# Moving the softplus remainder and the delta transposes, and plain DMAs for the mixtures' zero rows

## The reference, cut to what matters

```python
x = x + _L0_ffn_ref(_layernorm(x), ...)        # mixture: 8 experts, 2 for each token
x = x + _L1_attn_ref(_layernorm(x), ...)       # delta rule, 16 heads of 128
x = x + _L1_ffn_ref(_layernorm(x), ...)        # mixture: 8 experts, 2 for each token
# in the delta rule, for each head:
q, k, v = silu(short_conv(x @ W.T))            # three products, 4 taps
e = k @ Wsv.T - v                              # "guess errors"; their norms feed a small MLP
beta, amp = mlp_b(stats), mlp_a(stats)
g = -exp(A_log) * softplus(k / |k| * amp + dt_bias)
# recurrence over the tokens: S = S*exp(g); delta = (v - k.S)*beta; S += k x delta; o = q.S
```

## Time and profile before

| what | value |
|---|---|
| median of the runs | 7040.8 us (7029.47 to 7044.65, 3 runs) |
| profiled execution: its own time, its span | 7044.94 us, 7044.5 us |
| busy share of the span, PE / DVE / ACT / POOL | 81% / 74% / 54% / 40% |
| m0 from its first instruction to its end | 1334.5 to 1885.6 us |
| delta layer's preparation, up to the first projection | 1885.6 to 1995.1 us |
| delta loop, first to last decay | 2043 to 6043 us |
| m1 to the end | 6490.1 to 7044.5 us |

### The profile page before, as it was taken

One profiled execution on the slowest core, in us unless ns is written; L12 is line 12 of the kernel. 1 busy time (PEld: TensorE's weight loads), 2 busy tenths in 40 slices (PEclk: granted clock), 3 DMA queues, 4 the chain that ended last, 5 costly groups with the idle time before them and its releaser, 6 DMA issues. The chain is left out here.

```text
span 7044.5 us, 200500 instructions
## 1 busy us (share of the span) xinstructions
PE 5709.3 (81%) x69344; PEld 4012.6 (57%) x69345; DVE 5182.1 (74%) x11270; ACT 3800.4 (54%) x7867; POOL 2816.5 (40%) x4799
## 2 busy tenths in 40 slices
PE   6878999879167888888888888888888888688483
PEld 4767888645135555555555555555555555577342
DVE  6967777652347888888888888888888888555564
ACT  2324444212045676676676776766766767367121
POOL 2320000130325555555655555565556555200403
PEclk9979999889679999999999999999999999789697
DMA  1000000112300000000000000000000000001213
GB/s 34 0 17 7 4 5 5 44 47 86 84 10 15 16 13 16 16 16 13 13 16 16 16 13 16 13 16 16 16 13 13 16 16 11 11 12 58 75 63 100
DMA packets 136087, 172.77 MB, mean 25 GB/s; under 512 B 29104, under 2 KB 110096, under 8 KB 135184
## 3 DMA queue, kind: packets, MB, share of 16 engines
q1 hardware_dynamic: 122896, 135.34, 6.3%
q0 software_dynamic: 13056, 35.67, 1.6%
HBM read 128.74 MB, written 42.21 MB: 24 GB/s over the span
## 5 line engine op out<-in xcount | busy, mean ns | idle before, releaser
L2504 DVE TENSOR_TENSOR d_kq<-d_qkv,d_pre 128x512 f32<-128x512 f32 x768 | 526.9, 686 | 151.2 <-issue 147.7
L2469 DVE SCALAR_TENSOR_TENSOR d_y<-d_ps_kv,d_head,d_y 128x504 f32<-128x504 f32 (+2 forms) x768 | 560.8, 730 | 56.1 <-ACT d_y L2684 37.8
L2843 PE MATMUL d_ps_kv<-d_xnT,d_wqkv 128*128 (+1 forms) x1024 | 513.8, 625 | 34.9 <-issue 15.6
L1587 POOL MEMSET m_earlier<- 128x64 f32 x2 | 0.3, 152 | 1280.7 <-POOLq L3079 1280.7
L2921 PEld LDWEIGHTS d_ps_tx<-d_W,d_NT 64*64 64x64 f32 x10240 | 355.0, 135 | 233.1 <-issue 225.1
L2921 PE MATMUL d_ps_tx<-d_W,d_NT 64*64 64x64 f32 x10240 | 440.2, 225 | 30.0 <-DVE d_W L2552 17.1
L2347 POOL TENSOR_TENSOR d_roots<-d_radicand,d_power 128x20 f32<-128x20 f32 x128 | 459.5, 3590 | 10.0
L2908 PE MATMUL d_ps_level<-d_kq,d_ks 128*64 128x64 f32 x10240 | 440.6, 229 | 0.7 <-ACT d_vT L2648 0.7
L2676 ACT COPY d_T<-d_ps_tx 128x128 f32<-128x128 f32 x640 | 172.2, 269 | 480.1 <-PE d_ps_tx L2921 471.2
L2857 PE MATMUL d_ps_m<-d_prods,d_pick 128*32 128x512 f32 x2048 | 267.2, 641 | 169.5 <-ACT d_prods L2758 135.9
L2933 PE MATMUL d_ps_tx<-d_T,d_W 64*64 64x64 f32 x8192 | 346.8, 223 | 59.8 <-ACT d_T L2676 59.8
(11 more groups left out here) (467 smaller groups left out, 16426.2 us busy)
## 6 DMA issues: line engine op xcount, KB each, us to landing
d_wqkv<-in_d_wqkv SPq DMA_DIRECT2D x128, 384.0 KB, 3.1
m_xg<-m_rows_in SPq DMA_DIRECT2D x144, 128.0 KB, 2.0
m_rows_out<-m_ye SPq DMA_DIRECT2D x144, 128.0 KB, 1.7
b_ctx<-in_ctx SPq DMA_DIRECT2D x64, 128.0 KB, 2.0
d_wg<-in_d_wg SPq DMA_DIRECT2D x128, 64.0 KB, 2.6
x_sb<-in_x SPq DMA_DIRECT2D x8, 512.0 KB, 7.5
m_wgu<-in_m_wgu SPq DMA_DIRECT2D x2, 2048.0 KB
out<-x_sb SPq DMA_DIRECT2D x8, 512.0 KB
```

The lines of the kernel that those rows point to most:

```text
L2469: ins = nc.vector.scalar_tensor_tensor(out3, in3, head[A.i][:, tap:tap + 1], out3, ALU.mult, ALU.add)
L2504: nc.vector.tensor_tensor(dst, src, by, ALU.mult).then_inc(sems["kq_ready"], 1)
L2843: last = nc.tensor.matmul(ps_qkv[j], wqkv[u.i][:, j, kt, :], xnT[:, kt, tokens(u)], start=(kt == 0), stop=(kt == KT - 1))
```

## The change

- Delta loop, VectorE: `softplus_rest` leaves the end of the step; it is done one step later, as `softplus_rest(C)`, behind `errors(B)` and ahead of `taps(A, KEY)`. GpSimd: the first addition is now `rest` + Relu(z), and waits for the Relu (a new semaphore) and for `rest`; the second is `lnu` + `rest` and waits for the Ln.
- Delta layer's start: the normalising, turning and copying of the 32 tiles come ahead of the waits for the loads on all three engines; the preparation of the heads and ScalarE's Exp of the rates come behind it; TensorE waits for the loads before `g1` and for `heads_ready` before the loop.
- Mixtures: a region has 128 rows more, so a whole zero block can be written behind each expert's last token. VectorE works out the eight starts inside the last group's routing (two instructions); SyncE reads each start and writes 128 zero rows with a plain DMA. The lanes, the rows set aside (four GpSimd instructions), the eight VectorE instructions after routing and the eight indirect DMAs go.

```diff
-REGION = TOKENS
-CONSTANTS = 15
+REGION = TOKENS + P
+CONSTANTS = 11
-SPARE = ROWS + E * P
+SPARE = ROWS
@@ mixture, SyncE, behind the large loads
+                sp.wait_ge(sems["tails_ready"], 1)
+                for e in range(E):
+                    r = sp.value_load(tails[0:1, e:e + 1], min_val=0, max_val=ROWS - P)
+                    sp.dma_start(rows_in[bass.ds(r, P), :], zero[:, :]).then_inc(sems["spare_ready"], 16)
                 sp.wait_ge(sems["table_ready"], 1)
-                sp.wait_ge(sems["spare_ready"], 16)
-                sp.wait_ge(sems["scattered"], 16 * (PICKS * TILES + E))
+                sp.wait_ge(sems["spare_ready"], 16 * (E + 1))
+                sp.wait_ge(sems["scattered"], 16 * PICKS * TILES)
@@ mixture, GpSimd
-                pool.wait_ge(sems["tails_ready"], 1)
-                for e in range(E):
-                    nc.gpsimd.indirect_dma_start(out=rows_in, out_offset=bass.IndirectOffsetOnAxis(ap=tails[:, e:e + 1], axis=0),
-                                                 in_=zero[:, :], in_offset=None).then_inc(sems["scattered"], 16)
@@ mixture, VectorE, behind route(g)
+                    if g == GROUPS - 1:
+                        step(nc.vector.tensor_tensor(tail[:, :], so_far[:, TILES, :], region[:, :], ALU.add))
+                        step.settle()
+                        nc.vector.tensor_copy(tails[:, :], tail[:, :]).then_inc(sems["tails_ready"], 1)
@@ delta layer, GpSimd
                 def add_positive(B):
-                    pool.wait_ge(sems["ln_ready"], B.n)
-                    nc.gpsimd.tensor_tensor(lnu, lnu, z, ALU.add).then_inc(sems["pos_added"], 1)
+                    pool.wait_ge(sems["pos_ready"], B.n)
+                    hold(sems["soft_ready"], nth(B, 3, 2))
+                    nc.gpsimd.tensor_tensor(rest, rest, z, ALU.add).then_inc(sems["pos_added"], 1)
                 def softplus_sum(B):
                     pool.wait_ge(sems["pos_added"], B.n)
-                    hold(sems["soft_ready"], nth(B, 3, 2))
+                    hold(sems["ln_ready"], B.n)
                     nc.gpsimd.tensor_tensor(lnu, lnu, rest, ALU.add).then_inc(sems["soft_ready"], 1)
@@ delta layer, VectorE's start
                 dve.wait_ge(sems["rstd_done"], 1)
+                with dve.Fori(0, TILES // 2) as pair:      # y, L2452, with its wait for xT_ps
+                    ...
                 dve.wait_ge(sems["loaded"], 16 * len(loads))
                 ...
@@ VectorE's step
                     if B:
                         errors(B)
+                    if C:
+                        softplus_rest(C)
                     if A:
                         taps(A, KEY, 1)
...
-                    if B:
-                        softplus_rest(B)
                     if E and E.i == 1:
                         added(E, 1)
@@ ScalarE's start: behind the copies of the tiles instead of ahead of them
+                act.wait_ge(sems["loaded"], 16 * len(loads))
+                nc.scalar.activation(all_heads[:, :, NEGA], all_heads[:, :, NEGA], ACT.Exp).then_inc(sems["rates_ready"], 1)
@@ ScalarE, decay_logs
-                    nc.scalar.activation(z, z, ACT.Relu, bias=head_b[B.i][:, DT:DT + 1])
+                    nc.scalar.activation(z, z, ACT.Relu, bias=head_b[B.i][:, DT:DT + 1]).then_inc(sems["pos_ready"], 1)
@@ TensorE's start
-                pe.wait_ge(sems["loaded"], 16 * len(loads))
-                pe.wait_ge(sems["heads_ready"], 1)
                 ...                                        # the 32 transposes
+                pe.wait_ge(sems["loaded"], 16 * len(loads))
                 ...                                        # g1
+                pe.wait_ge(sems["heads_ready"], 1)
```

More of the change, by code:

```diff
@@ L1490, in mixture @@
         zero = mem.sbuf(f"{tag}_zero", [P, D])
-        aside_i = mem.sbuf(f"{tag}_aside_i", [P, E], I32)
-        lane_i, lane, aside = mem.sbuf(f"{tag}_lane_i", [P, 1], I32), mem.sbuf(f"{tag}_lane", [P, 1]), mem.sbuf(f"{tag}_aside", [P, E])
-        tail, inside, tails = mem.sbuf(f"{tag}_tail", [P, E]), mem.sbuf(f"{tag}_inside", [P, E]), mem.sbuf(f"{tag}_tails", [P, E], I32)
+        tail, tails = mem.sbuf(f"{tag}_tail", [P, E]), mem.sbuf(f"{tag}_tails", [P, E], I32)
         xn = mem.sbuf(f"{tag}_xn", [P, TILES, D])
@@ L1591, in _ @@
                 step(nc.gpsimd.memset(zero[:, :], 0.0))
-                step(nc.gpsimd.iota(lane_i[:, :], [[1, 1]], base=0, channel_multiplier=1))
-                step(nc.gpsimd.iota(aside_i[:, :], [[P, E]], base=ROWS, channel_multiplier=1))
                 step(nc.gpsimd.iota(count_i[:, :], [[1, NJ]], base=0, channel_multiplier=0))
@@ L1602, in _ @@
                 step(nc.gpsimd.tensor_copy(region[:, :], region_i[:, :]))
-                step(nc.gpsimd.tensor_copy(lane[:, :], lane_i[:, :]))
-                step(nc.gpsimd.tensor_copy(aside[:, :], aside_i[:, :]))
                 def scale(g):
@@ L1768, in _ @@
                 step(nc.vector.tensor_reduce(owner[:, :], passed[:, :, :], AX.X, ALU.add))
-                step(nc.vector.tensor_tensor(tail[:, :], so_far[:, TILES, :], lane[:, :].to_broadcast([P, E]), ALU.add))
-                step(nc.vector.scalar_tensor_tensor(inside[:, :], blocks[:, :], float(P), so_far[:, TILES, :], ALU.mult, ALU.subtract))
                 step.settle()
[L1772 to L1781, removed]
                 step(nc.vector.tensor_tensor(passed[:, :, :], passed[:, :, :], bcast_mid(blocks[:, 0:E - 1], NJ), ALU.mult))
@@ L2141, in delta_attention @@
             "featT_ps", "featT_ready", "hid_ps", "hid_ready", "mlp_ps", "mlp_ready", "zs_ready", "small_ready", "zs_ps", "z_ready", "abs_ready", "u_ready",
-            "ln_ready", "soft_step", "pos_added", "soft_ready", "decay_ready", "suf_ready", "late_ready", "diag_ready", "mask_ready", "vT_ps", "vT_ready",
+            "ln_ready", "soft_step", "pos_ready", "pos_added", "soft_ready", "decay_ready", "suf_ready", "late_ready", "diag_ready", "mask_ready", "vT_ps", "vT_ready",
             "kq_ready", "ks_ready", "level_step", "level_ps", "masked", "turned_first", "filled", "t_ps", "t_ready", "x_ps", "w_first", "w_sub", "w_step",
@@ L2437, in _ @@
                 dve.wait_ge(sems["rstd_done"], 1)
+                with dve.Fori(0, TILES // 2) as pair:
+                    for i in range(2):
+                        t = pair * 2 + i
+                        nc.vector.tensor_scalar(y[:, i, 0:D], x_sb[:, t, :], mv[:, t, 0:1], mv[:, t, 1:2], ALU.subtract, ALU.mult).then_inc(sems["xn_ready"], 1)
+                        if i == 1:
+                            dve.wait_ge(sems["xT_ps"], t + 1)
                 dve.wait_ge(sems["loaded"], 16 * len(loads))
@@ L2448, in _ @@
                 dve.wait_ge(sems["heads_ready"], 1)
[L2449 to L2454, removed]
                 dve.wait_ge(sems["g1_ready"], GROUPS)
@@ L2630, in _ @@
                 norm_stats_scalar(nc, act, mv, sems["std_ready"])
-                act.wait_ge(sems["loaded"], 16 * len(loads))
-                nc.scalar.activation(all_heads[:, :, NEGA], all_heads[:, :, NEGA], ACT.Exp).then_inc(sems["rates_ready"], 1)
                 banks = (ps_q, ps_level[0]), (ps_kv, ps_level[1])
```

## The result

The changed kernel ran in 6991.74 us (median of five, 6987.77 to 7007.83), the kernel before beside it in 7038.88 us: a ratio of 0.9938, 95% interval 0.9923 to 0.9952, 2.7 us above the 6989.0 predicted and inside the range. The interval stands for 34 to 54 us less and the medians are 47.1 us apart, where 51.8 was forecast; the kernel before had its median 1.9 us lower beside the change than when the forecast was made. The profiled execution took 6994.71 us with a span of 6992.7, against 7044.5 before: 51.8 us less.

What follows compares the result with a forecast made beforehand. No engine is full; a ring of waits through several engines paces the loop. Terms -33.3 - 8.9 - 9.6 + 0 = -51.8 us take the profiled 7044.94 to 6993.1, the median to 6989.0 us; range 6962 to 7008.

Steps and rivals of the forecast that it cites:

- Start: Delta layer's start: first y 0.42 us behind the reciprocal, train unchanged, loads and heads' preparation hidden; -33.3 us.
- m0: First mixture: the table ends last and sets the first fetch, at 1562.7 instead of 1571.56; -8.9 us.
- the gain is kept to the end: Both mixtures: the jobs behind the first fetch run as before, so none of the gain is lost.
- m1: Second mixture: first fetch at 6629.0 instead of 6638.57; -9.6 us, bounds -7.8 and -10.1.
- (a): Second mixture: the scatters end at 6625.98, so the first fetch could start at 6628.4.
- Loop: Delta loop: DVE's 0.9 us wait for u moves into waits for the guess, `next_w(D, 1)` and the decay; 0 us.
- the slack of 1.6 us: Delta loop: the softplus sum is there at 4068.43, ACT's decay Exp starts only at 4070.05.
- Rival 3: Delta loop: ACT comes to wait for the softplus sum, Exp 0.6 us late each step; +77 us, 7066 us, chance 0.03.
- my own two bounds: Delta loop: GpSimd's two additions end at 4068.5 to 4069.1 instead of 4068.43, slipping 0 to 0.6 us.
- the rule of the Trainium skill: DVE and GpSimd lock a shared port pair; beside idle GpSimd the remainder's first instruction gets about 0.28 us shorter on average.
- a DVE half and an ACT half: Delta loop: a ring of waits, DVE from `level_keys` to z, ACT from z through u to the next decay Exp.
- Rival 1: Delta loop: DVE is its bound, so 115 us more go; 6874 us, chance 0.06.

Runs made afterwards that it cites:

- e1: Only the delta layer's start changed, mixtures and loop as before, against the kernel before: 7010.60 us, ratio 0.9950.
- e3: Only the delta loop's softplus remainder and additions changed, against the kernel before: 7046.44 us, ratio 1.0003.
- e6: Changed kernel plus one 128x512 VectorE maximum and a wait for it per step, ahead of the KEY taps: 7006.68 us, ratio 0.9953 to the kernel before.
- e7: Changed kernel plus one 128x512 VectorE maximum and a wait for it per step, ahead of the VALUE taps: 7009.94 us, ratio 0.9964 to the kernel before.
- e8: Changed kernel with the softplus Relu moved from ScalarE to VectorE and the softplus remainders ahead of the guess errors: 6912.48 us, ratio 0.9823 to the kernel before.
- e4: Changed kernel with GpSimd's query-key product between its two softplus additions instead of behind them: 7064.18 us, ratio 1.0059 to the kernel before.
- e9: e8 with ScalarE's decay Exp moved ahead of the guess squares and the output's square: 7103.42 us, ratio 1.0079 to the kernel before.

## Why the prediction was right, and where only the sum was

**Start: right.** -33.7 us for -33.3, and every step of it: no DMA and no `heads_ready` holds anything. What I left out are 1.9 us behind it, in the table's fifth row, and 2.1 in e1 (50.3 us). Granted clock from 5 to 10 us behind the first projection, before and after:

```profile
2000.06:2005.06 5.00, 3.70 (x8) 1.44 (x8) 2.13 (x4) 1.74 (x3) 0.00 (x0) 1.00 0.04 6
```

```profile
1965.05:1970.05 5.00, 4.80 (x7) 2.03 (x8) 1.25 (x3) 0.69 (x1) 0.00 (x0) 0.66 0.00 0
```

The granted clock is the third number from the end: 0.66 instead of 1.00. The same eight wide products ran partly at 1.2 GHz in place of 2.4; two groups of four took 2.90 and 2.70 us instead of 1.98 and 1.88, all in all 1.7 us.

**m0: the term right, its keeping wrong.** "In both mixtures the jobs behind run as before, so the gain is kept to the end" is the step that failed: 3.3 of the 8.9 us were given back within the first jobs. From the first fetch to the seventh (the first that waits for a job's work) it took 19.4 us in place of 15.9, and then the jobs kept nearly the same step. TensorE's first weight products, before and after:

```profile
1575.75 2.71 PE L1997 MATMUL m_ps<-m_wgu,m_xgT 128*128 x4 [1.39 <-ACT m_xgT L1883]
...
1580.09 1.45 PE L1997 MATMUL m_ps<-m_wgu,m_xgT 128*128 x4 [1.21 <-ACT m_xgT L1883]
```

```profile
1571.19 2.71 PE L1983 MATMUL m_ps<-m_wgu,m_xgT 128*128 x4 [1.40 <-ACT m_xgT L1869]
...
1579.86 2.71 PE L1983 MATMUL m_ps<-m_wgu,m_xgT 128*128 x4 [0.77 <-ACT m_xgT L1869]
...
1584.70 1.45 PE L1983 MATMUL m_ps<-m_wgu,m_xgT 128*128 x4
```

The granted clock of stretches in it, before (two rows) and after (two rows):

```profile
1573.70:1578.20 4.50, 3.11 (x6) 1.65 (x7) 0.00 (x0) 0.37 (x1) 0.00 (x0) 0.50 0.39 117
1580.00:1583.00 3.00, 1.94 (x9) 1.20 (x9) 0.68 (x2) 1.80 (x6) 0.00 (x0) 1.00 0.14 44
```

```profile
1579.80:1582.50 2.70, 2.64 (x5) 1.53 (x6) 0.00 (x0) 0.00 (x0) 0.00 (x0) 0.50 0.00 0
1584.50:1590.00 5.50, 5.37 (x24) 3.18 (x22) 1.19 (x3) 1.33 (x6) 0.00 (x0) 1.00 0.23 72
```

Before, TensorE started again at 1573.70 after 20.7 us of rest, at 1.2 GHz, and was at 2.4 GHz by 1580. After, it started at 1569.13 after 11.0 us of rest, also at 1.2 GHz, and got to 2.4 GHz only at about 1584: two groups more at the slow level, at 1.26 us each, and their transposes. All nine kernels with the new mixture have these three slow groups, the three with the old one a single one. The rows show when the clock rose, not why so late.

**m1: right.** -10.0 us inside its bounds (-7.8 and -10.1), set by the scatters as (a) had it. The zero writes were fast (1.18 us apart, landing in 1.7 at the median).

**Loop: right in the size, wrong in two reasons.** The stall moved where I said it would, and nothing came of it (-1.2 us; 0.0 in e3). But the slack of 1.6 us was taken from the Exp itself. In the step of these rows, kind 0, what waits is the table load 1.30 us ahead of it: the slack was 0.23 us. In kind 1 the 1.6 us, less the wake-up, were there. Rival 3 would have begun at 0.23 in every second step, not at 1.6 in all, so its 0.03 was too little: with the upper of my own two bounds, GpSimd's sum 0.6 us later, kind 0 would have paid some 0.4 us. The measured slip was 0.1 us, because the remainder ran in 0.41 us. On that the rule of the Trainium skill that I weighed ("SBUF — State Buffer", "SBUF: two separate sides") held in direction: the instruction, with GpSimd idle beside it, took 416 ns on average (729 before: 1001 in kind 0, beside most of the mask product, and 457 in kind 1, beside its end), and e6 shows the other direction, GpSimd's addition 0.28 us longer, with 0.42 us of VectorE's operation on SBUF data beside it. As VectorE wasn't the bound, neither changed the time of this kernel. And "a DVE half and an ACT half" is only half of it: VectorE's half is laced with TensorE's inverse chain, and takes a quarter of what is put in; ScalarE's gave back 71 of the 93 us that were taken out.

**Rival 1** (VectorE is the bound) fell thrice: the loop didn't gain 115 us, e6 and e7 didn't lose 102, and e8 gained with more work on VectorE.

**The sum** came within 3 us of the median partly by luck. The terms give -52.6 us where -51.8 were forecast; the two losses at the clock (+3.3, +1.9) and a later start of m0 (+4.3) were then offset by stretches that I had down for nothing: -1.2, -2.1 and -5.4 us. The way from the start to m0's first fetch ran from 1558.3 to 1573.8 us in kernels with the new mixture and from 1571.6 to 1584.5 with the old: 13 to 15 us of scatter, nearly all of it from the code ahead of m0, the same in all (m0's first memset at 1330.6 to 1347.4 us). And the last stretch's -5.4 us is mostly chance: e1 and e3, with the old mixture too, have 402.3 and 402.0 us there, where the profiled kernel before had 405.9.

## What to carry to other kernels

Before you count on ScalarE's slack, look whether the wait stands ahead of the activation's table load or on the activation: in every second step here it stood ahead of the load, and 1.3 of the 1.6 us were not there. When a loop is a ring of waits, test which engine's queue it runs through before moving work: an operation of 0.73 us off the engine that is busy 70%, onto the one that is busy 85%, gave 79 us, where the same stall removed elsewhere gave none. And count, for an earlier start of TensorE, at which clock the work behind it will run.

## What the runs showed of the hardware

- A table load (1283 ns) needs no data, but it waits where the wait of its activation stands ahead of it: in kind 0 it started 0.09 us after the sum's end with 0.86 us of idle time before it (e4), in kind 1 it started 0.74 us before the sum's end (e9).
- A 128x512 VectorE maximum with both inputs in SBUF lengthened GpSimd's addition beside it from 1.27 to 1.55 us; VectorE's Relu in e8 took 1.27 us on average in the kind of step where it starts 0.25 us after GpSimd's mask product, and 0.52 us in the other, where that product is nearly over.
- Eight writes from SyncE, each with a value read ahead of it, went out 1.18 (m1) and 1.28 us (m0) apart, and freed GpSimd of eight indirect ones.
- TensorE came back to 2.4 GHz 6 us after its restart in one kernel and 15 us after it in the other, in the same code, after 21 and 11 us of rest; the kernels with the old mixture agree with the one, those with the new with the other.
